# Long GpSimd instructions of a three-stage language model kernel written as several shorter ones

## The reference

```python
h = tower(x)                              # 4 layers: layernorm, state-space scan, MLP with gelu; a last layernorm
h = h + attn(layernorm(h))                # 16 heads of 16: scores exp(-gamma * dist), masked, times v, Wo
h = h + ffn(layernorm(h))                 # 2 layers: local attention (8 heads of 64, window 128), gated MLP
```

## Time and profile before

| | before |
|---|---|
| time, median of 3 runs | 1275.93 us (1275.78 to 1276.22) |
| the profiled execution | 1278.31 us, its span 1276.4 us |
| TensorE busy (matmuls) | 1209.8 us, 95% |
| VectorE busy | 984.7 us, 77% |
| ScalarE busy | 860.2 us, 67% |
| GpSimd busy | 621.2 us, 49% |
| mean granted clock of TensorE | 0.983 of full |

### The profile page before, as it was taken

One profiled execution on the slowest core, in us unless ns is written; L12 is line 12 of the kernel. 1 busy time (PEld: TensorE's weight loads), 2 busy tenths in 40 slices (PEclk: granted clock), 3 DMA queues, 4 the chain that ended last, 5 costly groups with the idle time before them and its releaser, 6 DMA issues.

```text
span 1276.4 us, 26138 instructions
## 1 busy us (share of the span) xinstructions
PE 1209.8 (95%) x8899; PEld 1028.5 (81%) x8899; DVE 984.7 (77%) x2624; ACT 860.2 (67%) x1989; POOL 621.2 (49%) x678
## 2 busy tenths in 40 slices
PE   5999999999999999799978799999999999999998
PEld 3799988988888989577756567888888888888898
DVE  5767676666667777789878988888888888888754
ACT  2455766675556556689964668778777777777764
POOL 6523441361145243455434568556655567556543
PEclk9899999999999999899989999999999999999999
DMA  7400010001000000300110002000100000000001
GB/s 172 115 2 15 2 66 0 14 33 33 0 8 1 1 1 1 77 10 18 58 54 17 1 5 95 6 5 6 48 3 6 22 6 13 22 17 18 22 10 42
DMA packets 39615, 33.25 MB, mean 26 GB/s; under 512 B 16774, under 2 KB 36178, under 8 KB 39506
## 3 DMA queue, kind: packets, MB, share of 16 engines
q1 hardware_dynamic: 38610, 29.74, 7.7%
q0 software_dynamic: 768, 2.10, 1.0%
q10 hardware_dynamic: 128, 0.04, 0.0%
HBM read 25.84 MB, written 4.19 MB: 24 GB/s over the span
## 4 chain that ended last, share of the span: by engine, by line
PE 45%; DVE 6%; issue 3%; POOL 2%; ACT 2%; DVEq 0%; ACTq 0%; POOLq 0%
PE w_ps_p L1914 3%; PE w_ring L1975 3%; PE w_ring L1976 3%; PE w_ring L1873 3%; PE w_ring L1977 3%; PE w_ring L1875 3%; PE w_ring L1874 3%; PE w_ps_a L1932 2%; PE w_ring L1987 2%; PE a_ps L925 2%; PE w_ps_d L1907 2%; PE w_ps_d L1904 2%; PE w_ring L1891 2%; PE w_ring L1988 2%; PE w_ring L1991 1%
## 5 line engine op out<-in xcount | busy, mean ns | idle before, releaser
L392 ACT ACTIVATE t_gf<-t_ps_f,t_fb_cur 128x512 f32<-128x512 f32 x128 | 87.9, 687 | 159.8 <-PE t_ps_f L298 156.6
L542 DVE TENSOR_TENSOR t_g_lo<-t_gf,t_g_hi 128x512 fp32r<-128x512 f32 x128 | 93.3, 730 | 69.3 <-ACT t_g_hi L394 68.9
L311 PE MATMUL t_ps_o<-t_w_hi,t_g_hi 128*128 128x256 f32 x512 | 144.6, 282 | 0.1
L312 PE MATMUL t_ps_o<-t_w_lo,t_g_hi 128*128 128x256 f32 x512 | 143.0, 279 | 0.0
L313 PE MATMUL t_ps_o<-t_w_hi,t_g_lo 128*128 128x256 f32 x512 | 142.9, 279 | 0.0
L695 POOL TENSOR_TENSOR t_rs<-t_ve,t_neghalf 128x4 f32<-128x4 f32 x32 | 40.9, 1277 | 159.8 <-DVE t_ve L503 158.2
L296 PE MATMUL t_ps_f<-t_nh,t_w_hi 128*128 128x512 f32 x256 | 102.6, 401 | 1.5 <-DVE t_nl L518 0.8
L2988 POOL TENSOR_TENSOR w_m<-w_m 128x512 f32<-128x512 f32 x64 | 84.2, 1316 | 36.9 <-DVE w_m L2631 36.8
L298 PE MATMUL t_ps_f<-t_nl,t_w_hi 128*128 128x512 f32 x256 | 100.3, 392 | 0.0
L297 PE MATMUL t_ps_f<-t_nh,t_w_lo 128*128 128x512 f32 x256 | 100.0, 391 | 0.0
L311 PEld LDWEIGHTS t_ps_o<-t_w_hi,t_g_hi 128*128 128x128 f32 x512 | 96.2, 188 | 4.1 <-issue 0.9
(11 more groups left out here) (369 smaller groups left out, 4285.0 us busy)
## 6 DMA issues: line engine op xcount, KB each, us to landing
t_raw<-in_L_tok_w SPq DMA_DIRECT2D x8, 1024.0 KB, 5.4
out<-X SPq DMA_DIRECT2D x14, 256.0 KB, 2.2
raw<-in_L_ffn_wqkv SPq DMA_DIRECT2D x2, 1536.0 KB, 6.9
raw<-in_L_ffn_w SPq DMA_DIRECT2D x4, 640.0 KB, 4.8
w_raw_o<-out SPq DMA_DIRECT2D x8, 256.0 KB, 2.8
w_xs<-X SPq DMA_DIRECT2D x14, 127.0 KB
w_raw<-in_L_ffn_w SPq DMA_DIRECT2D x2, 640.0 KB
t_raw_d<-in_L_tok_D SPq DMA_DIRECT2D x4, 256.0 KB
```

The costliest lines, as they stand in the source:

```text
L311: pe.matmul(out, g_hi[:, j % 4, tok], w2_hi[:, j, :], start=(j == 0 and t % 2 == 0), stop=False, skip_group_check=True)
L312: pe.matmul(out, g_hi[:, j % 4, tok], w2_lo[:, j, :], start=False, stop=False, skip_group_check=True)
L392: act.activation(gf[:, j % 2, :], ps_f[:, j % 2, :], ACT.Gelu, bias=fb_cur[:, j:j + 1]).then_inc(pf_free, 1)
L542: dve.tensor_tensor(g_lo[:, j % 4, :], gf[:, j % 2, :], g_hi[:, j % 4, :].bitcast(F32), ALU.subtract).then_inc(g_split, 1)
```

## The change

Seven functions on GpSimd write their instruction as several over parts of the same columns. The semaphore that says that the whole is done is set by the last part, so what waits, and for what, stays as it was; so does the order. The parts have 128 to 426 columns, mostly 256. `scale_h` and `bias_h` no longer read the scale and bias through a broadcast over two tiles but once for each tile.

```diff
-                    pool.tensor_tensor(lo, whole, hi.bitcast(F32), ALU.subtract).then_inc(wa_l, 1)
+                    half_way = whole.shape[-1] // 2
+                    for cols in (slice(0, half_way), slice(half_way, 2 * half_way)):
+                        ins = pool.tensor_tensor(lo[:, cols], whole[:, cols], hi[:, cols].bitcast(F32), ALU.subtract)
+                    ins.then_inc(wa_l, 1)
...
-                pool.tensor_tensor(X[:, ST * s:ST * s + ST, :], xn[0][:, :, :], fs[:, :].unsqueeze(1).broadcast_to([P, ST, D]), ALU.mult).then_inc(h_mul, 1)
+                for t in range(ST):
+                    ins = pool.tensor_tensor(X[:, ST * s + t, :], xn[0][:, t, :], fs[:, :], ALU.mult)
+                ins.then_inc(h_mul, 1)
...
-                xs = X[:, ST * s:ST * s + ST, :]
-                pool.tensor_tensor(xs, xs, fb[:, :].unsqueeze(1).broadcast_to([P, ST, D]), ALU.add).then_inc(h_ready, 1)
+                for t in range(ST):
+                    xs = X[:, ST * s + t, :]
+                    ins = pool.tensor_tensor(xs, xs, fb[:, :], ALU.add)
+                ins.then_inc(h_ready, 1)
...
-                pool.tensor_tensor(wo_lo[:, :, :], raw_o[:, :, :], wo_hi[:, :, :].bitcast(F32), ALU.subtract).then_inc(S["split_o"], 1)
+                for c in range(IC):
+                    ins = pool.tensor_tensor(wo_lo[:, c, :], raw_o[:, c, :], wo_hi[:, c, :].bitcast(F32), ALU.subtract)
+                ins.then_inc(S["split_o"], 1)
...
-                pool.tensor_tensor(w2_lo[:, 0:FC - 1, :], raw_2[:, 0:FC - 1, :], w2_hi[:, 0:FC - 1, :].bitcast(F32), ALU.subtract).then_inc(S["split_2"], 1)
+                for j in range(FC - 1):
+                    ins = pool.tensor_tensor(w2_lo[:, j, :], raw_2[:, j, :], w2_hi[:, j, :].bitcast(F32), ALU.subtract)
+                ins.then_inc(S["split_2"], 1)
...
-                cols = slice(0, FULL + (UP + LAST) * u)
-                pool.tensor_tensor(w1_lo[:, :, u, cols], raw_1[:, :, u, cols], w1_hi[:, :, u, cols].bitcast(F32), ALU.subtract).then_inc(S["split_1"], 1)
+                end = FULL + (UP + LAST) * u
+                for c in range(DC):
+                    for cols in (slice(0, FULL // 2), slice(FULL // 2, end)):
+                        ins = pool.tensor_tensor(w1_lo[:, c, u, cols], raw_1[:, c, u, cols], w1_hi[:, c, u, cols].bitcast(F32), ALU.subtract)
+                ins.then_inc(S["split_1"], 1)
...
-                cols = slice(i * INNER, (i + 1) * INNER)
-                pool.tensor_tensor(qkv_lo[:, :, cols], raw_qkv[:, :, cols], qkv_hi[:, :, cols].bitcast(F32), ALU.subtract).then_inc(S["split_qkv"], 1)
+                for c in range(DC):
+                    for u in range(2):
+                        cols = slice(i * INNER + u * (INNER // 2), i * INNER + (u + 1) * (INNER // 2))
+                        ins = pool.tensor_tensor(qkv_lo[:, c, cols], raw_qkv[:, c, cols], qkv_hi[:, c, cols].bitcast(F32), ALU.subtract)
+                ins.then_inc(S["split_qkv"], 1)
```

## The result

The changed kernel takes 1281.42 us (median of 5 runs, 1280.57 to 1283.14) where the kernel before takes 1275.78 us (median of 5 runs on the same chip, 1272.61 to 1276.22). The ratio is 1.0053, with a 95% interval of 1.0036 to 1.0070: between 4.6 and 8.9 us slower. The forecast was 1275.7 us with a range up to 1279.1. Both the forecast and the range missed.

The account below looks back on a forecast made before the run. TensorE, busy 95% of the span, was taken as the bound, so GpSimd time counts only where TensorE waits for it. Seven places summed to -0.26, about -0.2 us: 1275.7 us from a median of 1275.93, range 1273.3 to 1279.1.

Parts of the forecast that it names:

- What a cut gives VectorE: A two-input SBUF VectorE instruction would wait for one 256-column GpSimd piece, 0.70 us, taking turns between queued pieces.
- Rival B: VectorE gets no turn between queued pieces and waits for the whole series: +2.7 us, 1278.6 us; chance 0.09.
- L716 row: Five 256-column L716 in a row took 5.32 us beside two L542; read as the two engines taking turns.
- (1): lo_2(1) at 1077: TensorE's 1.80 us wait and 1.7 us of clock go, a 1.6 us wait comes; gain 1.9.
- (2): lo_1(1, 1) at 1040: three more instructions and VectorE's turns on GpSimd's own chain; loss 0.55 us (0.4 to 0.9).
- (4): lo_o(0) at 732: begins GpSimd's chain to L3000, for which TensorE waits; loss 0.45 us (0 to 0.45).
- (3): lo_qkv(2) at 902: three more instructions lengthen TensorE's wait from 1.44 to 1.9 us; loss 0.45 us.
- rival A: The clock falls behind the new wait in (1) or (3): one fall 1277.4 us, chance 0.25; two 1279.1, 0.09.
- (5): lo_1(0, 1) at 764: of 0.45 us, 0.28 reach L2988, which holds VectorE's L2716; loss 0.28 us.
- (6): scale_h(0) at 465: L529, which TensorE waits for, is held less by L1464; gain 0.54 us (0 to 0.9).
- (7): scale_h between the attention stage's masks: one instruction more at 539, 577 and 595; loss 0.45 us (0 to 0.6).
- Rival C: GpSimd's lateness is hidden, in (1) (1274.1 us) or in (4), (5), (7) (1274.5), chance 0.11; both 1272.9, 0.04.

Follow-up runs that it names:

- experiment 9: Kernel before with bias_h cut in two and scale_h in four pieces of 128 columns: 1276.99 us, ratio 1.0004.
- experiment 12: Kernel before with only lo_o(0), lo_1(0,1) and lo_1(1,1) cut, in four each: 1273.16 us, one run.
- experiment 2: Kernel before with only scale_h cut in two, for all four sequences: 1275.62 us, ratio 1.0002.
- 1: Kernel before with only bias_h cut in two: 1281.21 us, ratio 1.0039.
- 7: Changed kernel with bias_h and lo_qkv(2) whole again: 1279.63 us, ratio 1.0032 against the kernel before.
- 8: Kernel before with only scale_h(0) cut in two and lo_2(1) in five: 1274.18 us, ratio 0.9992.
- 11: Kernel before, nothing cut, with a spare 64-column GpSimd write just ahead of scale_h: 1276.34 us, one run.
- 6: Kernel before with only lo_1(0,0) cut in four and lo_2(0) in five: 1272.77 us, one run.

## Why the prediction was wrong, step by step

- **What bounds the kernel, the price of a cut.** Right: 8.0 us more GpSimd time for 55 instructions.
- **What a cut gives VectorE.** Right: one piece and not the series, 0.76, 0.66 and 0.65 us at lo_2(1). Rival B falls, both there and by experiment 9, apart from w_sc (below). The L716 row it was weighed by shows five pieces of a series of eight.
- **(1) lo_2(1), -1.9.** The pair of traces says -1.87, with a new wait of 1.38 us for 1.6. But the term took the clock's fall of the one profile as certain. It is there in five of ten profiles; the cut itself gains 0.37 us, and on average about 1.1 us. A fall cost 1.5 us and not 1.7. The mechanism was right and the size wrong.
- **(2) lo_1(1,1), +0.55, and (4) lo_o(0), +0.45.** Right: 0.43 each (lo_o(0) from experiment 12). TensorE's wait behind lo_1(1,1) is now 0.97 us:

```profile
1054.51 0.55 PE L1921 MATMUL w_ps_p<-w_ident,w_pr 128*128 128x128 f32 x3 [0.97 <-POOL w_pr L3017]
```

- **(3) lo_qkv(2), +0.45, wait 1.9.** The cuts cost about 0.45 and the wait is 1.87 us, and then the clock fell, 1.5 us more (1.97 in all). That is rival A with one fall, held at 0.25.
- **(5) lo_1(0,1), +0.28.** It cost 0.72. Without the 0.50 us that w_sc is held longer 0.22 are left, so the 0.28 us of lateness were about right, and the step missed that w_sc, which began with the scaling of the probabilities, is held by it.
- **(6) scale_h(0), -0.54.** It gave 0.76. TensorE's wait of 1.47 us is now:

```profile
466.19 0.39 PE L283 MATMUL t_ps_t<-t_d_hi,t_nh 128*128 128x256 f32 x1 [0.93 <-DVE t_hs_cat L529]
```

- **(7) and bias_h.** The step whose mechanism failed. The prediction costed scale_h's cut at 0.45 us and every L1469 at nothing, "0.15 us for each further instruction where I am wrong". scale_h's cuts alone cost 0.27 us (experiment 2), so that was over-costed; the bias adds 1.7 us to that in the changed kernel and costs 3.64 us alone.
- **L2978 at 777 and L2973 at 782, at nothing.** 1.17 us. Each alone is free, as costed; together they exceed the idle time that hid them. The other places costed at nothing were free as far as the trace tells: over 400 to 450, 480 to 512, 810 to 890, 920 to 1030 and 1060 to 1075 the changed kernel's matmuls shift by 0.04 us or less.
- **Rival C** gives -1.2 as the sum without (4), (5) and (7). That is what these three add; the sum is -1.44, and the time beside it, 1274.5, is worked out from that.

The sum of the measured places (lo_o(0) as in experiment 12): -0.76 + 1.93 + 0.43 + 0.72 + 1.17 + 1.97 + 0.43 - 1.87 = +4.0 us against the profiled kernel before, which had the clock's fall at 1083; against one without it -0.37 stands for -1.87 and the sum is +5.5. The mean, 4.8 us, lies inside the measured 4.6 to 8.9, near its lower end; the ratio itself says 6.8 us, and what the 2 us between them are is not shown. The forecast's sum was -0.2. Of the gap of 5 us some 1.5 are (3)'s clock, 0.75 (1)'s, 1.5 the bias and the scale, 1.2 the pair at 777 and 782, 0.4 w_sc at 770.

The common fault is one premise: that lateness on GpSimd costs at most its own length, 0.15 us for an instruction, and only where TensorE already waits for GpSimd. The list of TensorE's waits shows who is late now, not who is ahead by 0.05 us. The row that would have told it was in the trace of before: a_ve at 559.87, scale_h at 559.92. I had looked for VectorE instructions with two inputs in SBUF alone. The Trainium skill, SBUF — State Buffer, "Who interferes with whom", also lists copy, cast and tensor_scalar as able to take the pair shared with GpSimd. The runs agree for tensor_scalar: a_ve and w_sc have one input, in SBUF, and were held 0.39 to 1.67 us.

**What stays open.** Whether the clock falls behind the wait of 1.8 us at 1083 differs from profile to profile, and no run here shows what decides it. It fell at other places too, at 541 in the kernel before (which lost 2 to 3 us there against most others), between 539 and 543 in 1, 7, 8 and 11, and at different points between 650 and 728 in every trace; I put none of that down to the change. Why w_sc was held through two instructions at 787 in the changed kernel and in 7 and at 780 in 6 (1.67, 1.67 and 1.63 us), but for one at lo_1(0,1) in the same changed kernel, in 7 and in 12 (0.66), is not settled. Experiment 7's ratio says more than its trace: its places sum to 1.2 us (lo_2(1) taken at the mean of 1.1), the ratio to 4.1 us (1.8 to 6.3). Part of that is the clock: the mean granted clock of its ten runs is 0.9847, that of the 19 runs of the kernel before 0.9864. A fall of 3.4 us takes 0.0013 off the mean and cost 1.5 us, so the difference stands for some 1.9 us (an estimate from these numbers). Why the clock fell more often in this kernel is open.

## What to carry over

Before adding time to an engine that is not the bound, list the short instructions of its partner that start just ahead of its own, with the margin. In this kernel an added 0.1 us that turned such an order cost the whole instruction that now went first. Check idle time against the sum of all the additions ahead of it, not against each. And treat a fall of the clock seen in one profile as a chance and not as a saving: look whether it is there in a second profile before putting it into a sum.

## What the hardware showed that was not expected

- A TENSOR_SCALAR of 2 columns with its one input in SBUF takes 0.17 us if it begins 0.01 us ahead of a GpSimd instruction of 512 columns, and 1.26 us if it begins 0.05 us behind it. The hold of a_ve lasts to the end of the GpSimd instruction it meets (0.39, 0.66, 1.22 us in all for 128, 256 and 2 x 256 columns).
- Between queued GpSimd pieces VectorE gets its turn in most cases, but w_sc waited through two of them in three traces (1.63 and 1.67 us).
- At 1083 a wait of TensorE of 1.8 us was followed by 1.2 GHz in five of ten profiles, at 906 one of 1.87 us in two of two and one of 1.44 to 1.46 us in none of twelve, behind lo_2(1) one of 1.38 us in none of four. But at 541 one of 1.36 us was followed by it in the kernel before. By these runs the length of the wait alone does not tell.
